# A fused Mamba and local-attention kernel: the q norm applied inside the exponential, softmax reciprocals widened by ScalarE

## The chip, the cores and the metric

The kernel runs on one core of a Trainium2 chip. The metric is the device time of one execution in microseconds. Its five engines run their own instruction streams, in the order in which the program issues them, and wait for each other through semaphores: PE (TensorE, matmuls; its weight loads are shown as PEld), DVE (VectorE), ACT (ScalarE), POOL (GpSimd) and SP, which only issues DMAs.

## What is computed

Two branches read the same normalised token rows (4096 tokens of width 256) and their results are added. The first is a Mamba block: a projection to 512 channels, a causal convolution with 4 taps, a recurrence with 16 states per channel over all 4096 tokens, a gate and a projection back. The second is two layers of windowed attention and a gated feed-forward. The attention part, cut to what the change touches:

```python
q = l2norm(q) * qs                      # l2norm(t) = t / clip(norm(t), 1e-12), per token and head
k = l2norm(k) * ksc
q, k = rotary_xpos(q, k)
...                                     # windows of 128; keys of own and previous window
sim = jnp.einsum('bhwid,bhwjd->bhwij', bq, bk)      # bq = q * 8
sim = jnp.where(mask, -jnp.finfo(sim.dtype).max, sim)
attn = jax.nn.softmax(sim, axis=-1)
out = jnp.einsum('bhwij,bhwjd->bhwid', attn, bv)
```

There are 8 heads of width 64. The q norm is one number per query row and head, so it commutes with the rotary step and with the product with k.

## The kernel before

Tokens go through in 8 chunks of 512. A chunk has 4 windows of 128 tokens and 2 layers, so 8 attentions, numbered `a` = 0 to 7; over the program there are 64. Everything is f32. Work on chunk c of the attention branch overlaps the Mamba recurrence.

The order on each engine is written out by hand as tables of words, one word for a step: `PE_ORDER`, `DVE_ORDER`, `ACT_ORDER`, `POOL_ORDER`, `SP_ORDER` for the six steady passes, and tables ending in `_FIRST` and `_LAST` for the first and the last pass. A word with a + belongs to the next chunk. A step waits for the semaphores of its inputs and of the buffers that it overwrites. TensorE's results go to a ring of 7 PSUM banks, taken in the order of the PE table.

The steps of one attention, with the line that does the work:

- `q(a)`, `k(a)`: TensorE projects to a bank, ScalarE squares it (L1017), VectorE sums the squares per head (L820) and forms the two rotary products (L830, L831, L834), a DMA issued by GpSimd adds them into `rot` (L1248), and GpSimd turns the sums into inverse norms `rnorm` by a maximum (L1236) and a power (L1239).
- `turn(q,a)`, `turn(k,a)` on ScalarE (`norm_heads`, L1036): each head's 64 columns of `rot` are multiplied by its inverse norm, 8 instructions for q and 8 for k.
- `heads(a)`: TensorE transposes k and then q (L1302), ScalarE copies them out (L1023, L1026).
- `s(a,c)`: TensorE adds mask and scores into two banks (L1402, L1408). `m(a,p)`: VectorE takes the negated row maxima `nmax` of one bank (L840). `e(a,g)`: ScalarE's exponential with `nmax` as bias, row sums accumulated (L1061).
- `pT(a,g)`: TensorE transposes the probabilities (L1302), ScalarE copies them out (L1069). `o(a,g)`: TensorE's product with V (L1429) into one bank of its own, `heads_out`.
- `rinv(a)`: VectorE inverts the row sums (L847). `rb(a)`: TensorE spreads them, by one matmul per head with `rinv` broadcast to 64 columns as the weights and the identity streamed (L1439), and ScalarE copies the result (L1075). `o(a)` on VectorE multiplies `heads_out` by it (L854). `wo(a)` projects back (L1452, L1454).

The rest of ScalarE's list is mostly `dA` (the recurrence's exponentials, L934); of VectorE's `scan` (L754, L761, L768).

## Time and profile before

| | us |
|---|---|
| median of three runs | 2109.19 |
| lowest, highest | 2108.12, 2111.52 |
| the profiled execution | 2109.78 |
| its span from first to last instruction | 2108.0 |
| TensorE busy | 1957.7 |
| VectorE busy | 1866.4 |
| ScalarE busy | 1675.6 |
| GpSimd busy | 1094.0 |

The profiled execution took 1.78 us more than its span, and 0.6 us more than the median. Busy time is the union of an engine's instructions, so it is smaller than the count times the mean duration where instructions overlap in the engine's pipeline, as matmuls do.

### The profile page before, as it was taken

The numbers are of one execution on the slowest core, as the hardware profiler recorded it, in microseconds if no ns is written. First come the engines' busy times: TensorE is split into PE (matmuls) and PEld (weight loads), VectorE is DVE, ScalarE is ACT, GpSimd is POOL, SyncE is SP. The second block draws the span as 40 slices with busy tenths as digits, with TensorE's granted clock in tenths as the row PEclk, the third lists the DMA queues.
The fourth block names the chain that finished last, engine by engine and source line by source line (L and its number), as shares of the span: only waits on it lengthen the run. The fifth ranks groups of instructions, "written<-read, shape, count | busy, mean of one in ns | idle before, by whom it ended". The sixth has DMA issues, their size and how long they took to land. (4 is left out here: it accounts for less than half of the span.)

```text
span 2108.0 us, 40069 instructions
## 1 busy us (share of the span) xinstructions
PE 1957.7 (93%) x12096; PEld 1341.7 (64%) x12096; DVE 1866.4 (89%) x2502; ACT 1675.6 (79%) x4124; POOL 1094.0 (52%) x1214
## 2 busy tenths in 40 slices
PE   6788999999999999999999999999999999998897
PEld 2465666666666666666675666666666666665666
DVE  3988999999999999999989999999999999898881
ACT  4866888878878888888879788897887888887672
POOL 3544554655545655555555555465554565545440
PEclk9989999999999999999999999999999999999999
DMA  4788899789896898888987898978889789788772
GB/s 159 175 216 194 185 245 226 179 194 239 193 250 169 189 250 191 220 200 216 225 213 192 199 222 219 229 190 201 233 197 251 171 194 247 163 212 214 205 150 53
DMA packets 131844, 425.26 MB, mean 202 GB/s; under 512 B 13584, under 2 KB 34832, under 8 KB 113072
## 3 DMA queue, kind: packets, MB, share of 16 engines
q0 software_dynamic: 64512, 184.58, 47.8%
q1 hardware_dynamic: 67120, 238.12, 33.8%
q8 instruction: 101, 1.65, 0.3%
q14 instruction: 111, 0.91, 0.1%
HBM read 241.76 MB, written 155.71 MB: 189 GB/s over the span
## 5 line engine op out<-in xcount | busy, mean ns | idle before, releaser
L761 DVE TENSOR_TENSOR_SCAN hb<-dA,state,hb 128x512 f32<-128x512 f32 x512 | 668.5, 1306 | 36.3 <-ACT dA L934 20.8
L1170 POOL DMA_DIRECT2D ysum<-dA x256 | 222.6, 878 | 375.4 <-DVE dA L768 343.8
L934 ACT ACTIVATE dA<-dt_sb,par 128x512 f32<-128x512 f32 x512 | 349.2, 729 | 12.4 <-DMA ysum<-dA 11.1
L1154 POOL COPY state<-hb 128x2 f32<-128x2 f32 x256 | 207.4, 810 | 255.4 <-DVE hb L761 255.4
L754 DVE TENSOR_TENSOR hb<-u_sb,bc 128x1024 f32<-128x1024 f32 x256 | 316.0, 1234 | 25.6 <-DMA bc<-bc_rows 11.5
L768 DVE TENSOR_TENSOR dA<-hb,bc 128x1024 f32<-128x1024 f32 x256 | 312.2, 1220 | 0.0
L1485 PE MATMUL ring<-hT,w 128*128 128x256 f32 x1280 | 294.9, 388 | 5.2 <-ACT hT L1082 4.1
L1036 ACT ACTIVATE rot<-rot,rnorm 128x64 f32<-128x64 f32 x1024 | 256.5, 341 | 45.1 <-POOL rnorm L1239 43.3
L1485 PEld LDWEIGHTS ring<-hT,w 128*128 128x128 f32 x1280 | 243.9, 193 | 56.3 <-ACT hT L1082 19.0
L1239 POOL TENSOR_TENSOR rnorm<-rnorm,powers 128x8 f32<-128x8 f32 x128 | 265.5, 2075 | 23.5 <-POOL rnorm L1236 22.2
L1061 ACT ACTIVATE probs<-ring,nmax 128x256 f32<-128x256 f32 x512 | 234.8, 481 | 34.5 <-DVE nmax L840 34.1
L1248 POOL DMA_DIRECT2D rot<-sq x128 | 116.3, 918 | 201.0 <-DVE sq L834 181.0
L1381 PE MATMUL ring<-wqkv,xnT 128*128 128x512 f32 x384 | 193.6, 631 | 1.2 <-issue 0.8
L1069 ACT ACTIVATE pT<-ring 128x512 f32<-128x512 f32 x256 | 146.9, 612 | 59.6 <-PE ring L1302 31.9
L1381 PE MATMUL ring<-wqkv,x2T 128*128 128x512 f32 x384 | 185.5, 613 | 2.5 <-ACT x2T L1113 2.5
L840 DVE TENSOR_REDUCE nmax<-ring 128x2 f32<-128x512 f32 x256 | 161.8, 681 | 25.6 <-PE ring L1408 24.9
L1504 PE MATMUL ring<-w,hid 128*128 128x256 f32 x768 | 176.5, 379 | 0.0
L1302 PE MATMUL ring<-ident,probs 128*128 128x128 f32 x1024 | 146.3, 284 | 23.2 <-ACT probs L1061 20.9
L1504 PEld LDWEIGHTS ring<-w,hid 128*128 128x128 f32 x768 | 145.8, 190 | 20.2 <-DVE hid L882 0.4
L1302 PEld LDWEIGHTS ring<-ident,probs 128*128 128x128 f32 x1024 | 117.3, 144 | 64.8 <-ACT probs L1061 32.6
L1429 PE MATMUL heads_out<-pT,V 128*64 128x128 f32 x2048 | 149.7, 282 | 3.3 <-ACT pT L1069 3.0
L1429 PEld LDWEIGHTS heads_out<-pT,V 128*64 128x64 f32 x2048 | 112.1, 138 | 61.6 <-issue 61.5
(122 smaller groups left out, 3536.9 us busy)
## 6 DMA issues: line engine op xcount, KB each, us to landing
bc<-bc_rows SPq DMA_DIRECT2D x128, 1024.0 KB, 6.0
ysum<-dA POOLq DMA_DIRECT2D x256, 512.0 KB, 7.3
rot<-sq POOLq DMA_DIRECT2D x128, 256.0 KB, 6.3
wqkv<-in_wqkv SPq DMA_DIRECT2D x48, 512.0 KB, 7.3
w<-in_w SPq DMA_DIRECT2D x16, 1408.0 KB, 11.2
w<-in_w SPq DMA_DIRECT2D x16, 896.0 KB, 10.8
tab<-in_tab SPq DMA_DIRECT2D x64, 128.0 KB, 8.4
wo<-in_wo SPq DMA_DIRECT2D x16, 512.0 KB, 9.9
```

What stands on the lines that cost most here:

```text
L754: dve.tensor_tensor(hb[:, slot:slot + 2, :], u_pair, bc[:, g % 2, :, 0, :], ALU.mult)\
L761: dve.tensor_tensor_scan(hb[:, k % H_RING, :], dA[:, k % DA_RING, :], hb[:, k % H_RING, :], state[:, k:k + 1], ALU.mult, ALU.add).then_inc ...
L768: dve.tensor_tensor(dA[:, out:out + 2, :], hb[:, slot:slot + 2, :], bc[:, g % 2, :, 1, :], ALU.mult).then_inc(hC_ready.sem, 1)
L934: act.activation(dA[:, k % DA_RING, :], dt_sb[:, j, :], ACT.Exp, scale=par[:, C_ALOG + n:C_ALOG + n + 1]).then_inc(dA_ready.sem, 1)
L1036: act.activation(rot[:, i, h * DH:(h + 1) * DH], rot[:, i, h * DH:(h + 1) * DH], ACT.Copy, scale=rnorm[:, i * HEADS + h:i * HEADS + h + 1] ...
L1061: act.activation(probs[:, g, odd, :], bank(it, ("s", a, p))[:, hh * 256:(hh + 1) * 256], ACT.Exp, bias=nmax[:, 2 * p + hh:2 * p + hh + 1], ...
L1239: pool.tensor_tensor(rnorm[:, part], rnorm[:, part], powers[:, part], ALU.pow).then_inc(rnorm_ready.sem, 1)
L1302: m = pe.transpose(bank(it, name)[:, b * P:(b + 1) * P], block_, ident[:, :])
L1381: m = pe.matmul(bank(it, name)[:, :], (x2T if l else xnT)[:, ft, off:off + WIN], wqkv[:, ft, i * 512:(i + 1) * 512], start=(ft == 0), stop ...
L1429: m = pe.matmul(obank[odd * DH:(odd + 1) * DH, g * WIN:(g + 1) * WIN], V[:, a // NW, s, h * DH:(h + 1) * DH], pT[:, g % 2, 2 * odd + s, :] ...
L1485: m = pe.matmul(out[:, part * 256:(part + 1) * 256], w1[:, ft, col:col + P], hT[:, ft, :], **edge)
L1504: m = pe.matmul(bank(it, ("w2", f))[:, v * D:(v + 1) * D], hid[:, i, toks], w2[:, i + v if last else i, :], start=False, stop=(i == NH - 1))
```

## The change

The q norm is no longer multiplied into `rot`. TensorE transposes q as soon as the DMA has added its halves. GpSimd computes the same inverse norms as before and keeps those of q in two slots by the parity of `a`. The exponential takes the row's inverse q norm as its `scale`, and as bias the negated maximum times that norm: VectorE forms it in `shifts` by a new step `mr(a,c)` (`scale_max`), twice per attention.

The reciprocals are spread in another way: a new ScalarE step `rinv(a)` (`widen`) writes each head's reciprocal 64 times into `rb`, TensorE transposes `rb` in four 128x128 blocks, and ScalarE copies the bank back into `rb` as before. The wait for the earlier `o` on VectorE moves from the copy to the widening.

All tables of orders are new. The core of the difference, with two lines of the first table:

```diff
-heads(7) +q(0) o(6,3) s(7,0) s(7,1) +k(0) pT(7,0) wo(6) pT(7,1) pT(7,2) o(7,0) pT(7,3) o(7,1) o(7,2) rb(7)
...
+o(6,3) heads(7) +q(0) s(7,0) s(7,1) +k(0) wo(6) pT(7,0) pT(7,1) pT(7,2) pT(7,3) o(7,0) o(7,1) rb(7) o(7,2)
...
-    rnorm = sb("rnorm", [P, 2 * HEADS])
+    rnorm = sb("rnorm", [P, 3 * HEADS])
+    shifts = sb("shifts", [P, HEADS])
-    normed = Signal("normed", 2 * HEADS * NA)
+    normed = Signal("normed", HEADS * NA)
+    shifts_ready = Signal("shifts_ready", 2 * NA)
+    widened = Signal("widened", NA)
...
+            def scale_max(a, c):
+                dve.wait_ge(*nmax_ready.at(it, a * PAIRS + 2 * c + 2))
+                dve.wait_ge(*rnorm_ready.at(it, 2 * a + 1))
+                dve.wait_ge(*probs_ready.at(it, (a - 1) * HEADS + 4 * c + 4))
+                part = slice(4 * c, 4 * c + 4)
+                slot = a % 2 * HEADS + 4 * c
+                dve.tensor_tensor(shifts[:, part].rearrange("p (o h) -> p o h", o=2),
+                                  nmax[:, part].rearrange("p (o h) -> p o h", o=2),
+                                  rnorm[:, slot:slot + 4].rearrange("p (h o) -> p o h", o=2), ALU.mult).then_inc(shifts_ready.sem, 1)
+
             def invert(a):
                 dve.wait_ge(*probs_ready.at(it, (a + 1) * HEADS))
-                dve.wait_ge(*filled(it if a else it - 1, ("rb", (a - 1) % NA)))
+                dve.wait_ge(*widened.at(it, a))
                 dve.reciprocal(rinv[:, :], rowsum[:, :]).then_inc(rinv_ready.sem, 1)
 
...
-                    "turn": rotate, "m": row_max, "rinv": invert, "o": heads_out,
+                    "turn": rotate, "m": row_max, "mr": scale_max, "rinv": invert, "o": heads_out,
...
-            def norm_heads(name, a):
-
-                i = "qk".index(name)
+            def norm_heads(a):
+
+                i = 1
                 n = 2 * a + i
                 act.wait_ge(*rot_added[i].at(it, D16 * (a + 1)))
                 act.wait_ge(*rnorm_ready.at(it, n + 1))
                 for h in range(HEADS):
                     act.activation(rot[:, i, h * DH:(h + 1) * DH], rot[:, i, h * DH:(h + 1) * DH], ACT.Copy,
-                                   scale=rnorm[:, i * HEADS + h:i * HEADS + h + 1]).then_inc(normed.sem, 1)
+                                   scale=rnorm[:, 2 * HEADS + h:2 * HEADS + h + 1]).then_inc(normed.sem, 1)
...
             def exps(a, g):
                 c, hh = divmod(g, 2)
-                act.wait_ge(*nmax_ready.at(it, a * PAIRS + 2 * c + 2))
+                act.wait_ge(*shifts_ready.at(it, 2 * a + c + 1))
                 act.wait_ge(*rinv_ready.at(it, a))
                 act.wait_ge(*filled(it if a else it - 1, ("pT", (a - 1) % NA, g)))
                 for odd in range(2):
                     p = 2 * c + odd
                     head = 2 * g + odd
                     act.activation(probs[:, g, odd, :], bank(it, ("s", a, p))[:, hh * 256:(hh + 1) * 256], ACT.Exp,
-                                   bias=nmax[:, 2 * p + hh:2 * p + hh + 1], accum_out=rowsum[:, head:head + 1])\
+                                   bias=shifts[:, 2 * p + hh:2 * p + hh + 1],
+                                   scale=rnorm[:, a % 2 * HEADS + head:a % 2 * HEADS + head + 1], accum_out=rowsum[:, head:head + 1])\
                        .then_inc(probs_ready.sem, 1)
...
+            def widen(a):
+
+                act.wait_ge(*rinv_ready.at(it, a + 1))
+                act.wait_ge(*oT_ready.at(it, a))
+                act.activation(rb[:, :, :].rearrange("p a (h d) -> p (a h) d", h=2),
+                               rinv[:, :].unsqueeze(2).to_broadcast([P, HEADS, DH]), ACT.Copy).then_inc(widened.sem, 1)
+
             def rb_out(a):
                 act.wait_ge(*filled(it, ("rb", a)))
-                act.wait_ge(*oT_ready.at(it, a))
                 act.activation(rb[:, :, :], bank(it, ("rb", a))[:, :].rearrange("p (a t) -> p a t", a=NJ), ACT.Copy)\
                    .then_inc(rb_ready.sem, 1)
...
@@ -1231,12 +1253,17 @@
                 part = slice(i * HEADS, (i + 1) * HEADS)
                 pool.wait_ge(*ssum_ready.at(it, n + 1))
                 pool.sem_inc(passed, 1)
-                pool.wait_ge(*normed.at(it, HEADS * (n - 1)))
-                pool.sem_inc(passed, 1)
-                pool.tensor_scalar(rnorm[:, part], ssum[:, part], 1e-24, None, ALU.max).then_inc(ssum_clipped.sem, 1)
+                if i:
+                    pool.wait_ge(*normed.at(it, HEADS * a))
+                else:
+                    pool.wait_ge(*probs_ready.at(it, HEADS * (a - 1)))
+                pool.sem_inc(passed, 1)
+                slot = 2 if i else a % 2
+                own = slice(slot * HEADS, (slot + 1) * HEADS)
+                pool.tensor_scalar(rnorm[:, own], ssum[:, part], 1e-24, None, ALU.max).then_inc(ssum_clipped.sem, 1)
                 pool.wait_ge(*ssum_clipped.at(it, n + 1))
                 pool.sem_inc(passed, 1)
-                pool.tensor_tensor(rnorm[:, part], rnorm[:, part], powers[:, part], ALU.pow).then_inc(rnorm_ready.sem, 1)
+                pool.tensor_tensor(rnorm[:, own], rnorm[:, own], powers[:, part], ALU.pow).then_inc(rnorm_ready.sem, 1)
...
             def heads(a):
                 for i, name in ((1, "kT"), (0, "qT")):
-                    pe.wait_ge(*normed.at(it, HEADS * (2 * a + i + 1)))
+                    if i:
+                        pe.wait_ge(*normed.at(it, HEADS * (a + 1)))
+                    else:
+                        pe.wait_ge(*rot_added[0].at(it, D16 * (a + 1)))
                     pe.wait_ge(*freed(it, (name, a)))
                     flip((name, a), [rot[:, i, p * P:(p + 1) * P] for p in range(PAIRS)])
...
             def spread(a):
-                pe.wait_ge(*rinv_ready.at(it, a + 1))
+
+                pe.wait_ge(*widened.at(it, a + 1))
                 pe.wait_ge(*freed(it, ("rb", a)))
-                for h in range(HEADS):
-                    g, odd = divmod(h, 2)
-                    m = pe.matmul(bank(it, ("rb", a))[odd * DH:(odd + 1) * DH, g * WIN:(g + 1) * WIN],
-                                  rinv[:, h:h + 1].to_broadcast([P, DH]), ident[:, :], start=True, stop=True)
-                m.then_inc(*done(it, ("rb", a)))
+                flip(("rb", a), [rb[:, g, :] for g in range(PAIRS)])
```

In the changed program VectorE has 128 instructions more (`shifts<-nmax,rnorm`), TensorE 256 transposes in place of 512 matmuls, ScalarE 512 multiplications of `rot` fewer and 64 widenings more, and 141 table loads in place of 146.

What moves is shown at three places of the first steady pass. Line numbers of the changed kernel are larger. Names are out<-in, and x counts equal instructions in a row.

TensorE around attention 7 of a chunk, before: the last transposes of the probabilities, the products with V with the spreading by L1439 among them, the back projection, the token shift, and the next chunk's transposes of `rot`.

```order
L1302 MATMUL ring<-ident,probs 128x128 x4
L1429 MATMUL heads_out<-pT,V 64x128 x8
L1439 MATMUL ring<-ident,rinv 64x128 x8
L1429 MATMUL heads_out<-pT,V 64x128 x4
L1452 MATMUL ring<-X,ident 128x256
L1454 MATMUL ring<-wo,oT 128x256 x4
L1466 MATMUL ring<-X,down 128x128
L1467 MATMUL ring<-xl,down 128x128
L1466 MATMUL ring<-X,down 128x128
L1467 MATMUL ring<-X,down 128x128
L1381 MATMUL ring<-wqkv,xnT 128x512 x2
L1302 MATMUL ring<-ident,rot 128x128 x8
```

And in the changed kernel:

```order
L1329 MATMUL ring<-ident,probs 128x128 x16
L1459 MATMUL heads_out<-pT,V 64x128 x8
L1329 MATMUL ring<-ident,rb 128x128 x4
L1459 MATMUL heads_out<-pT,V 64x128 x8
L1479 MATMUL ring<-X,ident 128x256
L1481 MATMUL ring<-wo,oT 128x256 x4
L1493 MATMUL ring<-X,down 128x128
L1494 MATMUL ring<-xl,down 128x128
L1493 MATMUL ring<-X,down 128x128
L1494 MATMUL ring<-X,down 128x128
L1408 MATMUL ring<-wqkv,xnT 128x512 x2
L1329 MATMUL ring<-ident,rot 128x128 x8
```

Eight matmuls from `rinv` have become four transposes from `rb` (now L1329 like all transposes), one pair of heads earlier among the products.

ScalarE around attention 2, before: `hn` from L1093 is the feed-forward's gelu, and the two groups at L1036 are the norms of q and of k of attention 3.

```order
L1051 ACTIVATE V<-ring 128x512
L934 ACTIVATE dA<-dt_sb,par 128x512 x3
L1093 ACT_TABLE_LOAD
L1093 ACTIVATE hn<-ring,par 128x256 x2
L1036 ACTIVATE rot<-rot,rnorm 128x64 x8
L1093 ACTIVATE hn<-ring,par 128x256 x2
L1036 ACTIVATE rot<-rot,rnorm 128x64 x8
L1093 ACTIVATE hn<-ring,par 128x256
L1093 ACTIVATE hn<-ring,par 128x128
L934 ACT_TABLE_LOAD
L934 ACTIVATE dA<-dt_sb,par 128x512
L1075 ACTIVATE rb<-ring 128x512
```

And in the changed kernel, where L1092 is the widening, L1085 the copy of the probabilities and L1097 the copy of the transposed `rb`:

```order
L1092 ACTIVATE rb<-rinv 128x512
L1085 ACTIVATE pT<-ring 128x512 x2
L1104 ACTIVATE hT<-ring,par 128x256 x2
L949 ACTIVATE dA<-dt_sb,par 128x512 x2
L1066 ACTIVATE V<-ring 128x512
L1097 ACTIVATE rb<-ring 128x512
L1115 ACT_TABLE_LOAD
L1115 ACTIVATE hn<-ring,par 128x256
L954 ACTIVATE xn<-xtok,shift,rstd 128x256 x2
L1115 ACTIVATE hn<-ring,par 128x256 x3
L1051 ACTIVATE rot<-rot,rnorm 128x64 x8
L1115 ACTIVATE hn<-ring,par 128x256
```

One group of 8 has gone, and the widening stands ahead of two copies of probabilities.

VectorE around the maxima of attention 2, before, with the rotary products of q of attention 3 between them:

```order
L761 SCALAR_TENSOR_TENSOR hb<-dA,state,hb 128x512
L768 TENSOR_TENSOR dA<-hb,bc 128x1024
L840 TENSOR_REDUCE nmax<-ring 128x2 x2
L820 TENSOR_REDUCE ssum<-sq 128x8
L830 TENSOR_TENSOR rot<-ring,tabs 128x8x32
L831 TENSOR_TENSOR rot<-ring,tabs 128x8x32
L834 TENSOR_TENSOR sq<-ring,tabs 128x512
L840 TENSOR_REDUCE nmax<-ring 128x2 x2
L761 SCALAR_TENSOR_TENSOR hb<-dA,state,hb 128x512
L754 TENSOR_TENSOR hb<-u_sb,bc 128x1024
```

And in the changed kernel:

```order
L766 SCALAR_TENSOR_TENSOR hb<-dA,state,hb 128x512
L773 TENSOR_TENSOR dA<-hb,bc 128x1024
L845 TENSOR_REDUCE nmax<-ring 128x2 x2
L825 TENSOR_REDUCE ssum<-sq 128x8
L835 TENSOR_TENSOR rot<-ring,tabs 128x8x32
L836 TENSOR_TENSOR rot<-ring,tabs 128x8x32
L839 TENSOR_TENSOR sq<-ring,tabs 128x512
L855 TENSOR_TENSOR shifts<-nmax,rnorm 128x4
L845 TENSOR_REDUCE nmax<-ring 128x2 x2
L855 TENSOR_TENSOR shifts<-nmax,rnorm 128x4
L766 SCALAR_TENSOR_TENSOR hb<-dA,state,hb 128x512
```

The same work stands there, with the two small products of L855 after the maxima.

## Rows read from the trace of the kernel before

**Rows 1.** The page: span, and busy time of each engine with its share and instructions.

```profile
span 2108.0 us, 40069 instructions
PE 1957.7 (93%) x12096; PEld 1341.7 (64%) x12096; DVE 1866.4 (89%) x2502; ACT 1675.6 (79%) x4124; POOL 1094.0 (52%) x1214
```

**Rows 2.** Busy time of each engine in four stretches; granted clock and DMA behind.

```profile
core 0: us, PE busy (x) PEld busy (x) DVE busy (x) ACT busy (x) POOL busy (x), PEclk, DMA share, GB/s
0.00:190.00 190.00, 142.15 (x747) 86.36 (x748) 137.74 (x184) 121.21 (x283) 85.39 (x109) 0.91 0.71 183
190.00:442.00 252.00, 239.90 (x1507) 164.84 (x1507) 232.34 (x314) 209.32 (x516) 133.34 (x148) 0.99 0.86 210
442.00:1697.00 1255.00, 1203.37 (x7573) 828.16 (x7575) 1164.26 (x1563) 1044.81 (x2577) 686.45 (x753) 0.99 0.86 210
1697.00:2108.00 411.00, 372.32 (x2276) 262.36 (x2268) 332.06 (x444) 300.21 (x750) 188.84 (x208) 0.96 0.73 179
```

**Rows 3.** Groups of TensorE: line, shapes, count | busy, mean ns | idle before, releasers.

```profile
L1439 PE MATMUL ring<-ident,rinv 128*64 128x128 f32 x1024 | 70.3, 280 | 1.8 <-DVE rinv L847 1.8
L1302 PE MATMUL ring<-ident,probs 128*128 128x128 f32 x1024 | 146.3, 284 | 23.2 <-ACT probs L1061 20.9 <-DVE hid L882 1.0 <-ACT V L1051 0.9
L1302 PE MATMUL ring<-ident,rot 128*128 128x128 f32 x512 | 70.2, 281 | 28.9 <-ACT rot L1036 27.6 <-ACT rb L1075 1.2
```

**Rows 4.** Timeline of TensorE: start, us, instructions [idle before <-releaser].

```profile
1124.87 0.60 PE L1302 MATMUL ring<-ident,probs 128*128 128x128 f32 x4
1125.31 1.88 PE L1381 MATMUL ring<-wqkv,xnT 128*128 128x512 f32 x4
1127.12 1.09 PE L1429 MATMUL heads_out<-pT,V 128*64 128x128 f32 x16
1128.04 1.04 PE L1439 MATMUL ring<-ident,rinv 128*64 128x128 f32 x16
1128.91 1.04 PE L1429 MATMUL heads_out<-pT,V 128*64 128x128 f32 x16
1134.92 1.09 PE L1302 MATMUL ring<-ident,rot 128*128 128x128 f32 x8 [2.60 <-ACT rot L1036]
```

**Rows 5.** Groups of ScalarE, columns as above.

```profile
L1036 ACT ACTIVATE rot<-rot,rnorm 128x64 f32<-128x64 f32 x1024 | 256.5, 341 | 45.1 <-POOL rnorm L1239 43.3 <-DMA rot<-sq 1.1
L1061 ACT ACTIVATE probs<-ring,nmax 128x256 f32<-128x256 f32 x512 | 234.8, 481 | 34.5 <-DVE nmax L840 34.1
L1082 ACT ACTIVATE hT<-ring,par 128x256 f32<-128x256 f32 x64 | 32.9, 570 | 4.9 <-PE ring L1302 4.9
L1075 ACT ACTIVATE rb<-ring 128x512 f32<-128x512 f32 x64 | 38.8, 607 | 16.9 <-PE ring L1439 16.9
L997 ACT ACTIVATE xconv<-xconv,par 128x512 f32<-128x512 f32 x32 | 21.5, 730 | 0.0
L934 ACT ACT_TABLE_LOAD x64 | 82.1, 1283 | 1.1
```

**Rows 6.** Groups of VectorE, columns as above.

```profile
L840 DVE TENSOR_REDUCE nmax<-ring 128x2 f32<-128x512 f32 x256 | 161.8, 681 | 25.6 <-PE ring L1408 24.9
L854 DVE TENSOR_TENSOR oT<-heads_out,rb 128x512 f32<-128x512 f32 x64 | 43.5, 680 | 14.4 <-PE ring L1454 7.0 <-issue 3.4 <-PE heads_out L1429 3.3
L847 DVE RECIPROCAL rinv<-rowsum 128x8 f32<-128x8 f32 x64 | 12.4, 194 | 6.7 <-ACT probs L1061 6.7
L874 DVE TENSOR_SCALAR mv<-mv 128x2 f32<-128x2 f32 x32 | 5.4, 169 | 1.1
```

**Rows 7.** Timeline of VectorE around one reciprocal.

```profile
1125.63 0.20 DVE L847 RECIPROCAL rinv<-rowsum 128x8 f32<-128x8 f32 x1
1125.74 0.64 DVE L854 TENSOR_TENSOR oT<-heads_out,rb 128x512 f32<-128x512 f32 x1
```

**Rows 8.** Timelines of GpSimd and ScalarE ahead of the longest TensorE wait.

```profile
1127.88 1.90 POOL L1239 TENSOR_TENSOR rnorm<-rnorm,powers 128x8 f32<-128x8 f32 x1 [0.18 <-POOL rnorm L1236]
1130.18 2.58 POOL L1239 TENSOR_TENSOR rnorm<-rnorm,powers 128x8 f32<-128x8 f32 x1 [0.18 <-POOL rnorm L1236]
1129.87 2.02 ACT L1036 ACTIVATE rot<-rot,rnorm 128x64 f32<-128x64 f32 x8 [0.78 <-POOL rnorm L1239]
1132.85 2.02 ACT L1036 ACTIVATE rot<-rot,rnorm 128x64 f32<-128x64 f32 x8 [0.95 <-POOL rnorm L1239]
```

338 lines of the change are left out of this document (170 added, 168 removed).

## The prediction

> **What bounds the kernel now.** I read the page first. TensorE is busy 1957.7 of 2108.0 us, VectorE 1866.4, ScalarE 1675.6, GpSimd 1094.0 [rows 1]. These averages mix the start, six steady passes and the end, so the second view cuts the span [rows 2]. In the middle, 442 to 1697 us, TensorE is busy 1203.4 of 1255 us (95.9%), VectorE 1164.3 (92.8%), ScalarE 1044.8 (83.3%). Two engines are nearly full there, TensorE the fuller, and no other resource is. At the start TensorE idles 47.9 us of 190, at the end 38.7 of 411. So a microsecond taken from TensorE is worth nearly one, as long as VectorE, with 90.7 us of slack in the middle, can follow; one taken from ScalarE is worth something only where another engine stands behind it.
>
> The third view is the waits of TensorE, by group [rows 3]: in the whole span it waited 27.6 us for ScalarE's norm of `rot` and 20.9 us for the exponentials. These are the two places where the change touches a chain that TensorE ends.
>
> **TensorE: the spreading becomes transposes.** Out go 1024 records of L1439, 70.3 us busy, 1.10 us per attention. In come 256 transposes of 128x128. Those of `rot` are the same form: 512 take 70.2 us, 0.137 us each [rows 3]; 256 make 35.1 us. That is a saving of 35.2 us. Busy time counts the pipeline's tail, so I take the other measure too, from start to start [rows 4]: the 16 records of one spreading hold TensorE from 1128.04 to 1128.91, 0.87 us; four transposes from 1124.87 to 1125.31, 0.44 us. 0.43 us by 64 is 27.5 us. I take the middle of the two, 31 us.
>
> **ScalarE: lighter, and off the bound.** The q norm leaves: 512 of the 1024 instructions of L1036, at 256.5/1024 = 0.25 us, 128 us. The widening comes: 64 instructions with 512 outputs. The trace has no copy that reads one element 64 times; the nearest are the copy from PSUM, 607 ns, and the scaled copy from SBUF, 730 ns, so 39 to 47 us, and I take 43. The exponential gets a second operand per row. No exponential here has both a scale and a bias from memory with 256 elements; L1082 has both, at 570 ns, against 481 ns for the exponential with its bias alone, so 89 ns by 512 are 46 us; the lower bound is nothing. Five table loads fewer at 1283 ns are 6 us [rows 5]. Together ScalarE loses 128 - 43 - 46 + 6 = 45 us of 1675.6. TensorE and VectorE, at 96 and 93%, cover it, so I count nothing on the path. If the exponential's 46 us lay open, they would eat the whole saving of TensorE.
>
> The row for this is thin, and a page prices the same thing: the Trainium skill, "ScalarE: Activation LUTs", section "What ACT_TABLE_LOAD costs", says that each pointer operand of an ACTIVATE adds about 93 ns. By it the exponentials would cost 48 us more in place of 46. It speaks against the change in the same way as the row does, and no run so far shows an exponential of this form.
>
> **VectorE: 128 products more.** Each reads 4 elements per row. The nearest rows are the reciprocal of 8 elements, 194 ns, and a two-element product that also waits for VectorE's own last result, 169 ns [rows 6]: 128 by 169 to 194 ns are 22 to 25 us busy. From start to start a reciprocal holds the engine for 0.11 us [rows 7], 14 us. I take 20 us, and must say how much of it shows. In the middle stretch 80 of the 128 fall, 12.5 us, and 40/64 of TensorE's 31 us, 19 us. Afterwards TensorE needs 1184 us and VectorE 1177: the two are equally full, and each must wait for the other more often. I let half of VectorE's 20 us through, 10 us; the bounds are 0 and 25. Where the product stands between maximum and exponential, behind it on VectorE are recurrence steps, and ScalarE's exponential waits for it: the 29 waits of ScalarE for the maxima, 34.1 us [rows 5], would each grow by some 0.2 us, 6 us, which lies within that half.
>
> **The path of q and k.** q reaches its transposes 2.02 us of ScalarE earlier. But look at the longest wait, 2.60 us at 1134.92 [rows 4]. GpSimd raises q's norms to the power from 1127.88 and k's from 1130.18 for 2.58 us; ScalarE multiplies q at 1129.87, has done by 1131.9, and idles 0.95 us until k's norms come; TensorE starts when k has been multiplied [rows 8]. ScalarE's q norm was in GpSimd's shadow, and GpSimd's work and its order of q before k stay. Of ScalarE's waits before L1036, 43.3 us are for these norms [rows 5]. So this wait stays, and I give the shorter path of q nothing.
>
> **The spreading's path.** Between reciprocal and result there is one more ScalarE instruction, 0.61 to 0.73 us [rows 5], less the 0.43 us that the transposes are shorter. VectorE's product at L854 waited 14.4 us in all and hardly for the copy [rows 6]; the work that hides it is the products with V and the projections that TensorE runs meanwhile. Nothing again, and the price without that cover is the third rival.
>
> **The new orders.** No wait of a row can be priced in an order that has not run. Idle time of 48 us at the start and 39 at the end [rows 2] could shrink or grow by a few us. I take nothing, with 8 us either way.
>
> **The sum.** 2109.8 (the profiled execution, which lies 0.6 us above the median) - 31 + 10 = 2088.8, so 2088 against the median of 2109.2: 1.0% faster.
>
> **Rivals.**
>
> More arrives. If VectorE's slack takes the products entirely and the shorter q path and lighter ScalarE take a third of TensorE's 48.5 us of waits for `rot` and the exponentials [rows 3], the time is 2109.8 - 31 - 16 = 2063; with 35 us saved it is 2059. For it speaks ScalarE's 45 us; against it that the two bounding engines come level.
>
> VectorE becomes the bound. Then its 25 us land whole and TensorE's saving turns into waiting: 2109.8 - 31 + 25 = 2104. For it speaks the 1177 against 1184 us; against it that VectorE still has 6% of slack.
>
> Slower: the widening blocks ScalarE. It waits for the reciprocal and for VectorE's earlier `o`, and in the order around attention 2 two copies of probabilities and a feed-forward copy are queued behind it, for which TensorE waits. If each of the 64 attentions puts one such copy of 0.7 us on TensorE's path, that is 45 us: 2109.8 - 21 + 45 = 2134. The point from which it decides is 21/64 = 0.33 us per attention. For it speaks that the three engines are in lockstep; against it that ScalarE idles 210 us in the middle.
>
> The transposes save nothing. If four of them did not overlap, each would cost its duration, 281 ns [rows 3], 256 would make 72 us, as much as is removed, and the sum would be 2109.8 + 10 = 2120. The eight at 1134.92 took 1.09 us together [rows 4], so they do overlap, and this gets 2%. Such a rule is in the Trainium skill: "TensorE: Matmul & The Clock Gate", section "Part 4: PE-mode transpose", gives some 275 ns for one in a kernel, dominated by access latency. The duration agrees with the trace; as a price for a row of them it does not.
>
> **How the numbers follow.** The forecast, 2080 to 2098, gets 40%; more arrives, 2055 to 2080, 21%; VectorE the bound, 2098 to 2105, 15%; these are all faster by over 0.2%, which is about what a measurement of this kernel can tell from no change: 76%. Mixtures that end within 0.2%, 2105 to 2113.4, get 8%. Slower gets 16%: 14% for the blocked ScalarE, 2113 to 2150, and 2% for the transposes. From 2062 to 2112 the range leaves out about 5% below and 15% above.
>
> **What the profile will show.** Right: 256 transposes from `rb` at 0.14 us busy each, TensorE busy near 1923 us; 128 products near 0.18 us; the exponential near 570 ns; TensorE's wait for k's norm still there; VectorE and TensorE equally full in the middle. Wrong: TensorE idle well over 165 us, with waits that end at the widening or at a copy of probabilities; or idle well under 150, which would mean that the shorter ScalarE work was worth more than I gave it.

## The result: slower by 1.2%

| | us |
|---|---|
| the changed kernel, median of 4 runs | 2133.65 (2131.86 to 2137.66) |
| the kernel before, median of 4 runs | 2108.65 (2106.87 to 2111.52) |
| ratio, 95% interval | 1.0116 (1.0096 to 1.0135) |
| forecast | 2088, range 2062 to 2112 |

The profiled execution took 2137.66 us, the longest of the four. Its page, span and busy time, answers to [rows 1]:

```profile
span 2135.9 us, 38274 instructions
...
PE 1942.9 (91%) x11328; PEld 1323.5 (62%) x11328; DVE 1878.3 (88%) x2630; ACT 1626.7 (76%) x3671; POOL 1078.8 (51%) x1214
```

Each engine has less or hardly more to do than before (TensorE -15 us, VectorE +12, ScalarE -49), and the span is 28 us longer: the time went into waiting. The same four stretches as in [rows 2], the last one longer by the added span:

```profile
0.00:190.00 190.00, 137.96 (x687) 82.38 (x688) 139.37 (x191) 121.60 (x262) 88.80 (x108) 0.90 0.67 178
190.00:442.00 252.00, 233.06 (x1356) 160.59 (x1355) 222.58 (x314) 192.84 (x435) 115.92 (x140) 0.96 0.83 204
442.00:1697.00 1255.00, 1181.03 (x7007) 807.37 (x7006) 1157.19 (x1626) 1005.34 (x2268) 675.93 (x746) 0.99 0.86 209
1697.00:2136.00 439.00, 390.81 (x2284) 273.16 (x2282) 359.14 (x502) 306.97 (x709) 198.11 (x221) 0.97 0.74 177
```

In the middle TensorE's busy time fell from 1203.4 to 1181.0 us, partly because less of the work falls into the same 1255 us now, and its idle time rose from 51.6 to 74.0. Counted from the first convolution of one pass to that of the next, a steady pass takes 254.5 us in place of 250.9, so the six of them make up some 21 of the 28 us. What TensorE waited for (us in total, times, longest):

```profile
PE ring L1329 <- ACT probs L1076: 37.7, 54, 3.2
PE ring L1329 <- ACT hn L979: 24.8, 23, 5.1
PE ring L1524 <- DMA w<-in_w: 21.2, 6, 4.1
PE ring L1329 <- ACT xn L954: 17.7, 2, 16.6
...
PE ring L1329 <- ACT rot L1051: 10.7, 5, 3.8
...
PE ring L1329 <- ACT rb L1092: 7.6, 7, 2.7
```

Against [rows 3]: the wait for the norms, now k's alone, fell from 27.6 to 10.7 us, that for the exponentials rose from 20.9 to 37.7, and two are new, for DMAs: the one shown and a single one of 3.2 us. The groups that the change made or touched (mean ns after the busy time):

```profile
L1076 ACT ACTIVATE probs<-ring,shifts,rnorm 128x256 f32<-128x256 f32 x512 | 281.4, 567 | 35.0 <-DVE shifts L855 34.6
...
L1051 ACT ACTIVATE rot<-rot,rnorm 128x64 f32<-128x64 f32 x512 | 128.8, 339 | 12.8 <-POOL rnorm L1266 12.2 <-DMA rot<-sq 0.6
...
L1092 ACT ACTIVATE rb<-rinv 128x512 f32<-128x512 f32 x64 | 40.9, 640 | 6.3 <-DVE oT L869 6.3
```

```profile
L1329 PE MATMUL ring<-ident,rb 128*128 128x128 f32 x256 | 40.9, 283 | 11.0 <-ACT rb L1092 7.6 <-ACT probs L1076 3.4
```

```profile
L855 DVE TENSOR_TENSOR shifts<-nmax,rnorm 128x4 f32<-128x4 f32 x128 | 26.5, 212 | 1.1
```

### The profile page after: what moved, and what is told of

Its sections match the earlier page's. It is cut to its first block and busy times, and to the rows that moved or that the text cites. A ratio compares the mean times of both kernels' runs of the same rounds, so it can differ in the third digit from the quotient of the medians.

```text
span 2135.9 us, 38274 instructions
## 1 busy us (share of the span) xinstructions
PE 1942.9 (91%) x11328; PEld 1323.5 (62%) x11328; DVE 1878.3 (88%) x2630; ACT 1626.7 (76%) x3671; POOL 1078.8 (51%) x1214
## 5 line engine op out<-in xcount | busy, mean ns | idle before, releaser
L1192 POOL DMA_DIRECT2D ysum<-dA x256 | 227.3, 918 | 392.5 <-DVE dA L773 343.3
L1176 POOL COPY state<-hb 128x2 f32<-128x2 f32 x256 | 233.3, 912 | 212.4 <-DVE hb L766 211.8
L1076 ACT ACTIVATE probs<-ring,shifts,rnorm 128x256 f32<-128x256 f32 x512 | 281.4, 567 | 35.0 <-DVE shifts L855 34.6
L1266 POOL TENSOR_TENSOR rnorm<-rnorm,powers 128x8 f32<-128x8 f32 x128 | 257.9, 2015 | 23.5 <-POOL rnorm L1263 21.8
L1408 PE MATMUL ring<-wqkv,xnT 128*128 128x512 f32 x384 | 188.4, 616 | 0.8 <-issue 0.8
L1531 PE MATMUL ring<-w,hid 128*128 128x256 f32 x768 | 187.5, 397 | 0.0
L1329 PE MATMUL ring<-ident,probs 128*128 128x128 f32 x1024 | 143.5, 280 | 35.1 <-ACT probs L1076 34.3
L1531 PEld LDWEIGHTS ring<-w,hid 128*128 128x128 f32 x768 | 154.2, 201 | 23.7 <-DVE hid L897 0.3
L1329 PEld LDWEIGHTS ring<-ident,probs 128*128 128x128 f32 x1024 | 115.2, 143 | 78.4 <-ACT probs L1076 53.6
L1032 ACT ACTIVATE sq<-ring 128x512 f32<-128x512 f32 x128 | 77.3, 605 | 113.1 <-PE ring L1408 112.4
L1085 ACT ACTIVATE pT<-ring 128x512 f32<-128x512 f32 x256 | 143.4, 610 | 19.4 <-PE heads_out L1459 15.6
L1459 PEld LDWEIGHTS heads_out<-pT,V 128*64 128x64 f32 x2048 | 112.4, 139 | 70.3 <-issue 65.1
```

The costliest lines, as they stand in the source:

```text
L1076: act.activation(probs[:, g, odd, :], bank(it, ("s", a, p))[:, hh * 256:(hh + 1) * 256], ACT.Exp, bias=shifts[:, 2 * p + hh:2 * p + hh + 1 ...
L1176: pool.tensor_copy(state[:, 2 * m:2 * m + 2], hb[:, slot:slot + 2, T - 1]).then_inc(state_saved.sem, 1)
L1266: pool.tensor_tensor(rnorm[:, own], rnorm[:, own], powers[:, part], ALU.pow).then_inc(rnorm_ready.sem, 1)
L1329: m = pe.transpose(bank(it, name)[:, b * P:(b + 1) * P], block_, ident[:, :])
L1408: m = pe.matmul(bank(it, name)[:, :], (x2T if l else xnT)[:, ft, off:off + WIN], wqkv[:, ft, i * 512:(i + 1) * 512], start=(ft == 0), stop ...
L1459: m = pe.matmul(obank[odd * DH:(odd + 1) * DH, g * WIN:(g + 1) * WIN], V[:, a // NW, s, h * DH:(h + 1) * DH], pT[:, g % 2, 2 * odd + s, :] ...
```

## The experiments

All ratios are against the kernel before on the same chip, whose median was 2106.8 to 2108.3 us. "Old orders" are the tables of the kernel before, "new orders" those of the change. Single executions of one kernel spread over up to 13 us, and the intervals reach some 3 to 6 us either way, so what is under 4 us is not told apart. Not all runs were made on the same chip: where a difference between two kernels is given below, it is that of their medians, and by the ratios of the table it comes out up to 4 us apart.

| run | orders | us | ratio, 95% interval |
|---|---|---|---|
| neither edit | new | 2146.72 | 1.0188 (1.0159 to 1.0216) |
| q norm edit | old | 2139.95 | 1.0161 (1.0137 to 1.0185) |
| spreading edit, widening 2 words ahead of the copy | old | 2198.67 | 1.0443 (1.0421 to 1.0465) |
| both edits, widening so | old | 2244.11 | 1.0656 (1.0625 to 1.0687) |
| changed kernel, load of w2 early | new | 2116.26 | 1.0045 (1.0027 to 1.0063) |
| q norm edit without scale pointer | old | 2122.01 | 1.0076 (1.0049 to 1.0102) |
| q norm dropped | old | 2106.03 | 0.9992 (0.9978 to 1.0006) |
| changed kernel without scale pointer | new | 2112.39 | 1.0031 (1.0015 to 1.0048) |
| spreading edit, widening at measured places | old | 2112.84 | 1.0022 (1.0007 to 1.0038) |
| the same, three spreadings a word later | old | 2122.95 | 1.0070 (1.0051 to 1.0089) |
| q norm edit | new | 2137.82 | 1.0143 (1.0120 to 1.0165) |
| spreading edit | new | 2148.62 | 1.0192 (1.0175 to 1.0209) |
| TensorE's short transposes alone | old | 2107.19 | 1.0002 (0.9986 to 1.0017) |
| the same and the widening, no hop | old | 2111.76 | 1.0022 (1.0006 to 1.0038) |
| two of four maxima over half the keys | old | 2091.16 | 0.9921 (0.9896 to 0.9947) |
| that and the short transposes | old | 2085.76 | 0.9897 (0.9869 to 0.9925) |
| no row maxima | old | 2051.32 | 0.9740 (0.9713 to 0.9766) |
| no row maxima, q norm edit | old | 2060.70 | 0.9767 (0.9744 to 0.9790) |

### Orders against edits

The first four kernels take the change apart: its tables without its edits, and its edits without its tables. A removed step's words leave the tables and an added step's words go in: `turn(q,a)` in front of `turn(k,a)`, `mr(a,c)` behind its second maximum, `rinv(a)` two words ahead of `rb(a)` on ScalarE (earlier where it would otherwise block a word that TensorE needs first).

```diff
 new orders, neither edit:  ... +dA +dA +turn(q,4) +turn(k,4) +hn(1) ...
 old orders, q norm edit:
-+m(0,0) +m(0,1) +turn(q,1) +m(0,2) +m(0,3)
++m(0,0) +m(0,1) +mr(0,0) +turn(q,1) +m(0,2) +m(0,3) +mr(0,1)
 old orders, spreading edit:
-+turn(k,3) +h(0,4) +h(0,5) +dA +rb(2)
++turn(k,3) +h(0,4) +rinv(2) +h(0,5) +dA +rb(2)
```

> The computation of before in the new orders (the q norm put back ahead of the k norm in ScalarE's table, the two new steps taken out). Theory A, the new orders cost the time and the edits save some: it must be slower than the changed kernel's 2134 us by what the edits save, 2145 to 2170 us, with TensorE's waits for the load of w2 (21 us in the changed kernel) still there. Theory B, the edits cost the time (the widening blocks ScalarE, or VectorE's 128 products become the bound): without them it comes back to 2100 to 2120 us.

> The q norm in the exponential alone, in the old orders (each product of the maxima right behind its second maximum, the q norm's word struck from ScalarE's table), the reciprocals spread as before. Theory A: ScalarE lighter by 128 - 46 = 82 us, VectorE heavier by 27 us, TensorE as before: 2100 to 2115 us. Theory B with VectorE as the bound: 2125 to 2137 us.

> The widening and the transposes of the reciprocals alone, in the old orders (the widening up to two words ahead of the copy of the bank, further where the old TensorE order asks for it), the q norm as before. Theory A: TensorE loses 29 us of busy time and the time falls to 2085 to 2105 us. Theory B, the widening blocks ScalarE: 2120 to 2150 us, with TensorE waiting for the widening or for copies of probabilities.

> Both edits in the old orders. Theory A: 2080 to 2105 us, the forecast that the prediction gave, since only the new orders are missing. Theory B: 2130 us or more, as slow as the changed kernel or slower, since the new orders were then what makes the edits bearable.

Measured: 2146.7, 2140.0, 2198.7 and 2244.1 us. Neither theory holds alone. The first time is theory A's and the fourth theory B's; the second lies 3 us above theory B's range and the third 49 us above it. The new tables cost the old computation 40 us (2146.72 against 2106.75 on the same chip), but they were laid out for other steps. In the old tables each edit costs. In the new tables both edits together take 13 us off the 2146.7, the q norm edit alone 9; the spreading edit alone gives nothing (2148.6). Nowhere do the edits bring the 21 us (31 less 10) of the forecast. So three things had to be found: what in the new tables costs, what the q edit costs, and why TensorE's shorter work brings nothing.

### The late load of w2

In the changed SP table the load of the down-projection's weights for layer 0, `+w2(0)`, stands behind `+q(3)`, `+v(3)` and `+k(3)`, which load the projection weights of layer 1 over those of layer 0. Before it stood ahead of `+bc(6)`. SP's issues in the kernel before, and then in the changed one:

```profile
1368.20 0.40 SPq L635 DMA_DIRECT2D w<-in_w  x1
...
1388.77 0.38 SPq L620 DMA_DIRECT2D wqkv<-in_wqkv  x1
```

```profile
1420.27 0.37 SPq L625 DMA_DIRECT2D wqkv<-in_wqkv  x1
...
1421.28 0.37 SPq L625 DMA_DIRECT2D wqkv<-in_wqkv  x1
1422.07 0.34 SPq L640 DMA_DIRECT2D w<-in_w  x1
```

The loads of `wqkv` can go only when TensorE has made attention 3's projections with the old weights, the last of which runs at 1418.30. The load of w2 behind them issues at 1422.07, 54 us later than before, of which some 22 (an estimate) are what the program lags by then (the pass began at 1216.8 in place of 1196.9), and TensorE stands at it (its timeline: start, duration, instruction, idle time ahead of it):

```profile
1418.30 1.88 PE L1408 MATMUL ring<-wqkv,xnT 128*128 128x512 f32 x4
...
1434.38 1.04 PE L1329 MATMUL ring<-ident,rot 128*128 128x128 f32 x8
1439.38 1.22 PE L1524 MATMUL ring<-X,ident 128*128 128x256 f32 x2 [3.96 <-DMA w<-in_w]
```

```diff
-+xres(0) ++x(0) +bc(6) store(1) +q(3) +q(4) +bc(7) +v(3) +v(4) +k(3) +w2(0) +v(5)
++xres(0) ++x(0) +bc(6) +w2(0) store(1) +q(3) +q(4) +bc(7) +v(3) +v(4) +k(3) +v(5)
```

> The changed kernel with one word of SP's order moved: the load of the first half of the down-projection's weights, +w2(0), issues right behind +bc(6), as in the kernel before, and no longer behind v(3), v(4) and k(3). Everything else is the changed kernel. Theory S (a good part of the loss is TensorE standing at that load once per pass, 21.2 us over six waits in the changed kernel's trace, none of them in the trace of before): the wait goes and the time falls by 15 to 22 us, to 2111 to 2119 us, with the wait for w<-in_w gone from TensorE's rows. Theory T (the wait only covers others: VectorE and ScalarE, 88% and 76% busy, use it to catch up): the wait goes from the rows, TensorE waits for ScalarE's probs and rb or for VectorE in its place, and the time stays at 2127 to 2136 us.

Measured 2116.26 us: 17.4 us from one word (it now stands behind `+bc(6)`, where before it stood just ahead of it), as theory S has it. By the ratios it is 15.0 us. The wait is gone from TensorE's rows; in its place stands one of 12.3 us for VectorE's part of the feed-forward (`hid`, in the last row of this section). The changed kernel with this word is still 0.45% slower than before, so the load is 60 to 70% of the loss, and some 8 us remain.

A second load is late in the new SP table, that of the second half of the next chunk's tokens: it issues at 1422.53, right behind w2, in place of 1367.22. VectorE waits for it once per pass, in the changed kernel and then with w2 early, where the kernel before has 7.3 us in two waits:

```profile
DVE stats L799 <- DMA xtok<-in_x: 28.5, 6, 5.1
```

```profile
DVE stats L799 <- DMA xtok<-in_x: 15.6, 6, 2.8
```

No run moves this load alone, so what it is worth is open.

TensorE also runs slower after the wait for w2. The windows of the changed kernel around it (PE busy, PEld, DVE, ACT, POOL, granted clock, DMA share, GB/s):

```profile
1430.00:1436.00 6.00, 5.42 (x42) 4.39 (x40) 4.46 (x7) 3.95 (x13) 3.59 (x4) 1.00 1.05 285
1436.00:1440.00 4.00, 0.62 (x2) 0.53 (x3) 0.10 (x1) 3.03 (x4) 0.79 (x3) 0.72 1.05 341
1440.00:1445.00 5.00, 5.00 (x14) 4.03 (x13) 4.87 (x11) 1.32 (x3) 1.84 (x3) 0.54 0.75 196
1445.00:1450.00 5.00, 5.00 (x32) 3.80 (x30) 4.48 (x4) 2.34 (x6) 1.70 (x2) 1.00 0.66 102
```

After 3.96 us of idling the granted clock of the next 5 us is 0.54, so 1.2 GHz, the lower of its two levels, for most of them, and matmuls of w2 that come there take up to 634 ns in place of 379 (the columns are the least, median and greatest duration):

```profile
L1531 PE MATMUL ring<-w,hid x24: 379/379/634, 1440.4 to 1447.9; 128*128 128x256 f32 x24
```

In the whole trace this group, and below it the same group with the load early, has a mean of 397 and 384 ns against 379 before. Between the two profiles TensorE's idle time falls by 10 us (193.0 to 182.8) and its busy time by 11 (1942.9 to 1931.8), 7 of them in this group:

```profile
L1531 PE MATMUL ring<-w,hid 128*128 128x256 f32 x768 | 187.5, 397 | 0.0
```

```profile
L1531 PE MATMUL ring<-w,hid 128*128 128x256 f32 x768 | 180.4, 384 | 12.3 <-DVE hid L897 12.3
```

### What the q norm edit costs

Three kernels in the old orders, the q norm edit and two that take from it, differ by one thing each: the pointer, then VectorE's step as well. In the latter two, and in the run in the new orders, q is not normalised.

```diff
 without scale pointer (old orders; the same edit in the new ones):
-   bias=shifts[...], scale=rnorm[...], accum_out=...
+   bias=nmax[...], accum_out=...
 q norm dropped, in addition:
-   +mr(0,0) ... +mr(0,1)          act.wait_ge(*shifts_ready...)
+                                  act.wait_ge(*nmax_ready...)
```

> Old orders, q norm edit alone as in the earlier run of it (2139.95 us), with VectorE's shifts still computed and still waited for, but the exponential takes no scale pointer and its bias from nmax: q is then not normalized at all (left out of the computation). Only the 86 ns per exponential (512 of them, 44 us of ScalarE) differ from that run. Theory P (the exponentials stand between TensorE's scores and its probs transposes, and their added time lies open there): the time falls by 15 to 40 us, to 2100 to 2125 us, and TensorE's wait for probs falls from 33.8 to about 20 us. Theory O (the q norm edit costs by the shifts' extra step on VectorE and by the moved waits for POOL's rnorm): the time stays within 6 us of 2140.

> Old orders, q norm dropped altogether: neither ScalarE's eight scalings of q nor VectorE's shifts nor the scale pointer are there; the exponential's bias is nmax, as before, and q is not normalized (left out of the computation). Theory P (the exponentials' added time is the q edit's cost): 2075 to 2100 us, what 128 us less of ScalarE work is worth when nothing is put in its place; the difference to the run without the pointer, the price of VectorE's shifts, is 5 to 15 us. Theory O: the difference between the two is over 20 us. If the removed scalings are worth nothing (they lie beside other work), it stands at 2100 to 2112 us.

> The changed kernel (new orders, both edits), but the exponential takes no scale pointer and its bias from nmax, so q is not normalized (left out of the computation); VectorE's shifts stay and are still waited for. Theory P: the exponentials' 44 us lie open in the new orders as well, and the time falls by 15 to 30 us, to 2104 to 2119 us. Theory T (the new orders are bound elsewhere, by the load of w2 and by k norm's chain): it falls by under 8 us, to 2126 or more.

Measured 2122.01, 2106.03 and 2112.39 us. In the old orders, step by step: the eight scalings of q removed (with the waits of TensorE and GpSimd changed for it), -1.5 us, within the noise; VectorE's shifts and the exponential's wait for them, +16.0; the exponential's second pointer, +17.9. In the new orders the pointer costs 21.3 (17.9 by the ratios). Theory P stands in both orders, though dropping the norm gains nothing, so its 2075 to 2100 us for that run were missed and 2100 to 2112 came true, and the shifts cost a little more than its 5 to 15 us. The first number is the forecast's own argument about GpSimd's powers: with 122 us less to do, ScalarE waits at L1045 for k's norms, 108.9 us in place of 43.3 for q's and k's [rows 5], and TensorE's wait for ScalarE's norms stays, 25.0 us in place of 27.6.

```profile
ACT rot L1045 <- POOL rnorm L1253: 108.9, 37, 5.1
```

TensorE's waits for the exponentials, with the norm dropped, with the shifts, and with shifts and pointer:

```profile
PE ring L1316 <- ACT probs L1070: 17.7, 21, 4.5
```

```profile
PE ring L1320 <- ACT probs L1074: 22.3, 26, 4.7
```

```profile
PE ring L1321 <- ACT probs L1074: 33.8, 37, 4.9
```

They grow step by step, by 16 of the 34 us. In all TensorE's idle time grows by 23 us from the first profile to the last (152.6 to 175.2), and its busy time by 7 (1954.6 to 1962.0). The shifts are seen at work on ScalarE too: its exponentials wait 33.2 us for the maxima in the first run and 42.7 for the shifts in the second.

### What the widening costs, by its place

```diff
 widening at measured places (ScalarE, old orders):
-+turn(k,3) +h(0,4) +rinv(2) +h(0,5) +dA +rb(2)
++turn(k,3) +rinv(2) +h(0,4) +h(0,5) +dA +rb(2)
 and three spreadings a word later (TensorE):
-o(7,2) rb(7) o(7,3)    +rb(5) +o(5,0)    +rb(6) +pT(6,2)
+o(7,2) o(7,3) rb(7)    +o(5,0) +rb(5)    +pT(6,2) +rb(6)
```

> Old orders, spreading edit alone, as in the earlier run of it (2198.67 us), but ScalarE's widening word stands where the trace of before shows VectorE's reciprocal just ended, one to 15 ScalarE words (31 in the last pass) ahead of where the copy of rb stands. Theory W (the earlier run lost its 92 us because the widening stood two words ahead of the copy, behind ScalarE words that started long after the reciprocal, and TensorE waited for it): TensorE's wait for rb falls from 119.2 us to under 35 us, and the time to 2095 to 2125 us. Theory H (the hop itself, reciprocal to widening to transposes, is what costs, since the spreading stands 0.2 to 1 us behind the reciprocal in three of eight attentions): the time stays above 2150 us.

> As the one before it, with TensorE's spreading moved one word later in three attentions where it had stood right at the reciprocal: rb(7) behind o(7,3), +rb(5) behind +o(5,0), +rb(6) behind +pT(6,2). Theory W with the hop open at those three (0.5 to 1.2 us each per pass): 5 to 20 us under the run without this move, and by then at or under before (2080 to 2110 us), since 20 us of TensorE work are gone. Theory V (the copy of rb, and the attention output on VectorE behind it, then come later instead): within 4 us of the run without the move, or slower.

> New orders with the late load of w2, q norm edit alone (transposes and copy of before). Beside it stand the run with neither edit in the new orders (2146.7 us) and the changed kernel (2133.7 us). Theory Q (the q norm edit costs in the new orders what it costs in the old ones, some 33 us, and the spreading edit earns it back and more): 2160 us or more. Theory N (the new orders were laid around the q norm's hop, so the edit costs little there): 2135 to 2155 us.

> New orders with the late load of w2, spreading edit alone, with the q norm back on ScalarE in front of k's. Theory Q: the spreading edit earns its 22 us of TensorE time and more in orders that leave room for its hop: 2105 to 2128 us, under the changed kernel. Theory N (the q norm's scalings, 128 us of ScalarE, find no room in orders laid without them): 2134 us or more.

Measured 2112.84, 2122.95, 2137.82 and 2148.62 us. Theory W stands: the same instructions cost 92 or 5 us, by where one word per attention stands in ScalarE's table. TensorE's wait for the widening, first with it two words ahead of the copy, then at the measured places:

```profile
PE ring L1310 <- ACT rb L1078: 119.2, 49, 9.7
```

```profile
PE ring L1310 <- ACT rb L1078: 18.7, 24, 2.9
```

Moving three spreadings out of the way of the hop made it 10 us slower, theory V; what is late next there I did not follow. In the new orders the edits are worth: q norm -9 us, spreading +2, both -13. Both numbers are theory N's. The time of the second run can't say, though, that the missing room for q's scalings is its reason. TensorE's waits for ScalarE's norms speak for it. In the new orders with neither edit, with the spreading edit, and with the q norm edit they are:

```profile
PE ring L1302 <- ACT rot L1036: 40.8, 27, 5.1
```

```profile
PE ring L1310 <- ACT rot L1038: 40.8, 26, 4.5
```

```profile
PE ring L1321 <- ACT rot L1049: 12.3, 5, 5.3
```

So where the tables leave no room for q's scalings, the q norm edit takes 28 us of waiting away, which in the old orders (27.6 to 25.0 us) it does not.

### What a microsecond of each engine is worth

The spreading edit with its widening well placed takes 23 us of TensorE's busy time away and gains nothing. Four runs ask for the marginal price directly.

```diff
 short transposes alone (softmax division left out):
-   m = pe.matmul(bank(...)[...], rinv[:, h:h + 1].to_broadcast([P, DH]), ident[:, :], ...)   # x8
+   flip(("rb", a), [ident[:, :] for g in range(PAIRS)])
 half the keys in two of four maxima:
+   keys = WIN if p % 2 == 0 else 2 * WIN
-   bank(it, ("s", a, p))[:, :].rearrange("p (h k) -> p h k", h=2)
+   bank(it, ("s", a, p))[:, :].rearrange("p (h k) -> p h k", h=2)[:, :, 0:keys]
 widening without hop:
+   act.activation(wide[...], rinv[:, :].unsqueeze(2).to_broadcast([P, HEADS, DH]), ACT.Copy)
```

> The kernel before, old orders, with only TensorE's part of the spreading edit: four 128x128 transposes per attention in place of the sixteen narrow matmuls, in the same place and behind the same wait for VectorE's reciprocal, but of the identity and not of widened reciprocals (the softmax division is left out, no widening, no hop). TensorE has some 22 us less work. Theory E (TensorE is the bound, as the prediction had it): 2082 to 2092 us. Theory C (work of TensorE, ScalarE and VectorE is chained, and TensorE time taken away there turns into waiting): 2098 to 2108 us.

> The run before with ScalarE's widening added at the measured places, into a tile that nobody reads: its 0.64 us of ScalarE, 64 times, are there, but TensorE does not wait for it (the softmax division is left out). Beside the run with the widenings in the same places and the hop (2112.8 us) it separates the price of the work from that of the hop. If the work costs: 10 to 25 us above the run without widenings. If the hop costs: within 5 us of that run, and 8 us or more below 2112.8.

> The kernel before, old orders, with the row maximum taken over half the keys in two of the four maxima of each attention (part of the maximum is left out): 128 of them take some 0.41 in place of 0.68 us, 34 us less of VectorE's work, on the way from TensorE's scores to the exponentials. Theory E (TensorE bounds, VectorE has slack): the time falls by under 8 us. Theory C (chained): by 15 to 34 us.

> Both: TensorE 22 us less, VectorE 34 us less (softmax division and part of the maximum left out). Theory E: the sum of the two single runs' savings, nearly all TensorE's. Theory C: both together save clearly more than the two alone added (one alone leaves the other's chain standing), 2055 to 2080 us.

The pages of the run with the short transposes alone, and of the one with the cheaper maxima:

```profile
span 2099.4 us, 38533 instructions
...
PE 1931.2 (92%) x11328; PEld 1313.4 (63%) x11328; DVE 1868.1 (89%) x2502; ACT 1675.5 (80%) x4124; POOL 1079.3 (51%) x1214
```

```profile
span 2085.3 us, 40069 instructions
...
PE 1943.6 (93%) x12096; PEld 1335.2 (64%) x12096; DVE 1828.1 (88%) x2502; ACT 1674.6 (80%) x4124; POOL 1101.8 (53%) x1214
```

| taken away | engine's busy time | the time |
|---|---|---|
| TensorE's narrow matmuls | -26.5 us | -0.3 us (-3.0 to +3.6) |
| half of two maxima, VectorE | -38.3 us | -16.3 us |
| both | -31.2, -38.1 us | -21.8 us |
| ScalarE's q norm (the run above) | -122.3 us | -1.5 us |

TensorE, 93% busy, gives nothing back for 26 us, and theory E falls. The single profiled execution of that run had a span of 2099.4 us; its ten timed runs have a median of 2107.19, and these decide. Both together save 21.8 us, 5 more than the two alone add up to, which the noise allows to be nothing, so the strong form of theory C, 2055 to 2080 us, falls too. The widening's work without the hop costs 4.6 us (2111.76; the two intervals overlap), and the hop 1.1 us more (2112.84), within the noise. That fits neither expectation in full: work alone was to cost 10 us or more, and the hop 8. Where the widening is well placed the hop costs nothing that I can measure.

### A version that beats both

q and k are normalised, so on these inputs the scores stay in the range of an f32 exponential, and the maxima can go altogether; a softmax is the same for any shift. With other learned scales of q and k one would have to bound the scores first.

```diff
-                act.wait_ge(*nmax_ready.at(it, a * PAIRS + 2 * c + 2))
+                act.wait_ge(*filled(it, ("s", a, 2 * c)))
+                act.wait_ge(*filled(it, ("s", a, 2 * c + 1)))
-                                   bias=nmax[:, 2 * p + hh:2 * p + hh + 1], accum_out=...
+                                   accum_out=...
```

> The kernel before, old orders, without the row maxima: the 256 reductions of VectorE (161.8 us) are gone, the exponential has no bias and waits for TensorE's scores directly. q and k are normalised, so the scores stay small enough for an f32 exponential on these inputs, and a shift by a constant leaves the softmax what it is; the computation is complete for them. VectorE's half of a chain between scores and exponentials goes with its load. Theory C (VectorE stands beside TensorE as a bound, 34 us less of it were worth 16 us): the first part of the 162 us is worth half, until TensorE is full alone; 51.6 us of TensorE's idle time in the middle and some of the 87 us at start and end can go: 2030 to 2070 us. Theory E (TensorE the bound, the 16 us were a part at the ends): 2085 us or more.

> The same with the q norm edit, old orders: ScalarE's eight scalings of q are gone, the exponential has the inverse q norm as its scale and no bias, so one pointer as before, and VectorE has no shifts. This is the q edit without its two prices (16 us for the shifts, 18 us for the second pointer). Computation complete for these inputs. If the 128 us of ScalarE are worth nothing because k's norm comes last on that chain in any case: within 5 us of e_no_max. If they are worth something once VectorE is light: 6 to 20 us under it.

Measured 2051.32 us, 2.6% faster than before, in the old orders. VectorE has 153 us less to do, and ScalarE 48 less, since the exponential has lost its only pointer; together they are worth 57 us, and no run parts the two. TensorE's middle is now 97.6% busy; theory C's range holds. Page, windows and exponential:

```profile
span 2047.8 us, 39812 instructions
...
PE 1931.0 (94%) x12096; PEld 1335.5 (65%) x12096; DVE 1713.2 (84%) x2246; ACT 1628.0 (79%) x4124; POOL 1082.8 (53%) x1214
```

```profile
442.00:1697.00 1255.00, 1224.32 (x7837) 852.34 (x7836) 1099.38 (x1441) 1047.50 (x2663) 695.89 (x773) 1.00 0.88 218
```

```profile
L1056 ACT ACTIVATE probs<-ring 128x256 f32<-128x256 f32 x512 | 187.6, 397 | 4.7 <-PE ring L1403 4.7
```

With the q norm edit it takes 2060.70 us. Both guesses of the expectation missed: the edit does not gain, it seems to cost 9 us, though the two intervals overlap. The expectation was also wrong in saying "one pointer as before": the other kernel's exponential has none. With one it takes 89 ns longer:

```profile
L1066 ACT ACTIVATE probs<-ring,rnorm 128x256 f32<-128x256 f32 x512 | 234.5, 486 | 5.2 <-PE ring L1421 5.1
```

## Why the prediction was wrong

**"So a microsecond taken from TensorE is worth nearly one."** This step failed, and with it the sum's main term, -31 us. The work itself shrank nearly as forecast: the spreading's group fell from 70.3 to 40.9 us (35.1 forecast), and the busy time from 1957.7 to 1942.9 (1923 forecast); 11 us of what is missing are longer matmuls of w2, 187.5 in place of 176.5 us, 7 of them due to the late load. But the transposes alone, which take 26.5 us of busy time away, gain 0.3 us of time. A busy share of 96% was read as a bound. The 51.6 us of idle time in the middle are waits at certain places, and work taken away between two such waits only makes the second longer: in the run with the short transposes alone TensorE's middle idled 61.9 us.

```profile
442.00:1697.00 1255.00, 1193.12 (x7109) 811.48 (x7102) 1168.10 (x1563) 1045.59 (x2583) 676.23 (x753) 0.99 0.86 210
```

Over the whole span its idle time grew from 150.3 to 168.2 us. Among the waits that grew are those ahead of the back projection (13.2 us before, the releaser not seen), those for the gelu, new at this place, and those for the norms (27.6 before):

```profile
PE ring L1302 <- ACT rot L1036: 30.0, 21, 2.7
...
PE ring L1448 <- issue: 18.2, 17, 3.5
...
PE ring L1381 <- ACT hn L964: 6.2, 6, 1.0
```

**"They cover it, so I count nothing on the path"** (the exponential's pointer). Its duration was right, 567 ns against 570. The cover was not: it costs 17.9 us in the old orders and 21.3 in the new. The prediction said that open it would eat TensorE's whole saving; it is open for some 40 to 50%.

**VectorE, +10 us.** The instruction takes 212 ns in place of 169 to 194, 26.5 us busy in place of 20, and costs 16 us in the old orders. The mechanism was named; the term was too small, though inside its bounds of 0 to 25.

**The path of q and k, nothing.** Right in the orders that the rows showed: the whole ScalarE norm of q is worth 1.5 us there, within noise, behind GpSimd's norms of k. In the new orders it does not carry over: with q's scalings in place TensorE waited 40.8 us for the norms, without them 12.3, and in the changed kernel 10.7, where the prediction had the wait stay.

**The spreading's path, nothing.** Right only as far as the order is right: 1 us at measured places, 92 with the widening two words ahead of the copy. In the changed kernel TensorE waits 7.6 us for it.

**The new orders, nothing, with 8 us either way.** This step failed by more than its margin: the new tables cost the computation of before 40 us, and the late load of w2 alone costs the changed kernel 17.4. It could have been read before the result: SP's table was in the change, and `load_wqkv` waits for attention 3's projection.

**The rivals.** The blocked ScalarE came out at the measured number, 2134 us, but that is luck: ScalarE idled 6.3 us ahead of the widening in the whole trace, and the load and the exponentials made the loss. It also took TensorE's saving as real. The sign of being wrong did come: TensorE idled 193 us, well over 165. But the places it named, the widening (7.6 us) and the copies of probabilities (6.4 us), were not the main ones. "VectorE the bound" was nearer to the cause, but gave 2104 us at most.

**What the loss consists of.** The load, 17.4 us, and the pointer, 21.3, are measured in the changed kernel. The shifts, 16.0, the widening, 4.6, and the removed scalings, -1.5, are measured in the old orders. Added up they make 58 us, and the change costs 25. So the rest must give back some 33 us. One place where it does so can be named: in the new orders the q norm edit as a whole gains 9 us although the pointer's 21 are in it, so what else it does there gives back some 30 us, an estimate, and TensorE's wait for the norms is 28 us shorter. The sum that needs no prices from the old orders is this: the tables cost 40 us, and the two edits in them give back 13 to 15. Differences of this kind are not measurements, and single prices need not add up.

**What is still open.** The three things that cost or gain (maxima 0.43 us per us of work, shifts 0.57 on 28 us, the pointer 0.39 on 46 us, in the old orders) all stand between TensorE's scores and its transposes of the probabilities; the three that are worth nothing (q's scalings, the narrow matmuls, and at 0.11 the widening) stand elsewhere. ScalarE has 20% of slack, and 122 us less of its work gave nothing, so the pointer can hardly cost through load. That this chain sets the time fits all of it. But for VectorE's part load and chain were not parted: no run takes as much off VectorE elsewhere. The late load of the tokens was not tested either.

## What to carry to other kernels

Where several engines are about 80% busy or more, the busiest need not be the bound: here 26 us less work on an engine that was 93% busy gave nothing. Price an edit by whether its instruction stands on the chain that the waits run through, and test it with a kernel that only leaves the work out. An instruction moved between engines needs its word in the table where its input is just ready; a word's place was worth some 86 us here, more than any edit. Read the DMA queue's order in a change first: one load behind three that wait for TensorE's projections made 15 to 17 of the 25 us of loss, and TensorE came out of the wait that is shown at its lower clock.
